# Router choices stored compactly and spread out by GpSimd in the expert stage, and router scores for two tiles at once

## What is computed

```python
logits = einsum('bgtd,des->bgtes', grouped, controller) + tie
perm = (logits == max(logits, axis=t))          # 1.0 or 0.0
dispatched = einsum('bgtd,bgtes->bgesd', grouped, perm)
inner = relu(einsum('bgesd,desf->bgesf', dispatched, f1) + bias)
intermediate = einsum('bgesf,esfd->bgesd', inner, f2)
out = einsum('bgesd,bgtes->bgtd', intermediate, perm)
x = layernorm(x + out)
```

## Time and profile before

| | us |
|---|---|
| median of 3 executions | 2290.38 |
| range of them | 2289.61 to 2296.89 |
| profiled execution, its own time | 2293.73 |
| its span, first to last instruction | 2291.9 |

### The profile page before, as it was taken

How to read it: one execution, slowest core, us unless ns; L and a number is a source line. 1 busy time by engine, 2 the same in 40 slices (tenths; PEclk the granted TensorE clock), 3 DMA queues, 4 the chain that set the end, 5 groups by cost and what they waited for, 6 DMA issues and landing times. The chain is left out here.

```text
span 2291.9 us, 35132 instructions
## 1 busy us (share of the span) xinstructions
PE 1934.8 (84%) x12598; PEld 1322.7 (58%) x12598; DVE 1405.0 (61%) x2695; ACT 940.8 (41%) x1751; POOL 443.1 (19%) x283
## 2 busy tenths in 40 slices
PE   7999999999999799999789999993767676576444
PEld 6777777777777343444378888883636362252000
DVE  5887778777877354555478889874434354354344
ACT  4444444444444344544345555552323232232222
POOL 1100100010000143554355554530000000000000
PEclk9999999999999899999989999995889887787555
DMA  5233333333422588887587777757798999989999
GB/s 169 74 122 118 113 109 132 112 111 111 138 102 93 171 221 231 222 222 221 158 259 245 239 243 222 238 169 258 248 389 290 390 348 407 404 305 408 375 392 345
DMA packets 306173, 522.66 MB, mean 228 GB/s; under 512 B 27119, under 2 KB 125583, under 8 KB 297682
## 3 DMA queue, kind: packets, MB, share of 16 engines
q1 hardware_dynamic: 296786, 503.63, 65.1%
q10 hardware_dynamic: 9216, 16.78, 1.9%
HBM read 314.50 MB, written 205.82 MB: 227 GB/s over the span
## 5 line engine op out<-in xcount | busy, mean ns | idle before, releaser
L89 PE MATMUL p_pu<-p_xT_high,p_win_high 128*128 128x512 f32 (+1 forms) x816 | 334.8, 410 | 13.5 <-DVE p_win_low L84 13.3
L91 PE MATMUL p_pu<-p_xT_low,p_win_high 128*128 128x512 f32 (+1 forms) x816 | 318.3, 390 | 0.0
L90 PE MATMUL p_pu<-p_xT_high,p_win_low 128*128 128x512 f32 (+1 forms) x816 | 318.3, 390 | 0.0
L422 ACT ACTIVATE p_t<-p_pu,p_tbias,p_taps 128x512 f32<-128x512 f32 x192 | 149.4, 778 | 383.4 <-PE p_pu L91 382.5
L536 DVE SCALAR_TENSOR_TENSOR p_t<-p_pu,p_taps,p_t 128x384 f32<-128x384 f32 (+1 forms) x384 | 210.3, 548 | 6.8
L808 POOL TENSOR_TENSOR q_y<-q_y 128x512 f32<-128x512 f32 x128 | 160.7, 1277 | 191.7 <-DVE q_y L829 191.7
L84 POOL TENSOR_TENSOR p_xT_low<-p_xT,p_xT_high 128x2048 fp32r<-128x2048 f32 (+1 forms) x17 | 75.8, 4458 | 616.7 <-ACT p_xT_high L79 616.7
L89 PEld LDWEIGHTS p_pu<-p_xT_high,p_win_high 128*128 128x128 f32 x816 | 155.0, 190 | 46.6 <-POOL p_xT_low L84 11.5
L91 PEld LDWEIGHTS p_pu<-p_xT_low,p_win_high 128*128 128x128 f32 x816 | 154.3, 189 | 34.3
L90 PEld LDWEIGHTS p_pu<-p_xT_high,p_win_low 128*128 128x128 f32 x816 | 155.1, 190 | 27.2
L1406 PE MATMUL e_pd<-e_taken,e_ff 128*32 128x128 f32 x2048 | 86.8, 324 | 96.7 <-DMA e_ff<-in_L_ffn_f 93.0
(11 more groups left out here) (123 smaller groups left out, 3754.1 us busy)
## 6 DMA issues: line engine op xcount, KB each, us to landing
s_I<-e_out SPq DMA_DIRECT2D x64, 1024.0 KB, 8.2
s_SV<-p_sout SPq DMA_DIRECT2D x128, 256.0 KB, 2.0
q_av<-s_SV SPq DMA_DIRECT2D x64, 512.0 KB, 4.3
s_Z<-q_z SPq DMA_DIRECT2D x128, 256.0 KB, 3.2
o_zin<-s_Z SPq DMA_DIRECT2D x64, 512.0 KB, 3.7
e_ff<-in_L_ffn_f SPq DMA_DIRECT2D x64, 512.0 KB, 9.0
e_inter<-s_I SPq DMA_DIRECT2D x32, 1024.0 KB, 12.8
e_taken<-s_I SPq DMA_DIRECT2D x32, 1024.0 KB, 11.7
```

The costliest lines, as they stand in the source:

```text
L89: pe.matmul(out, a[0], b[0], start=start, stop=False)
L90: pe.matmul(out, a[1], b[0], start=False, stop=False)
L91: return pe.matmul(out, a[0], b[1], start=False, stop=stop)
L422: nc.scalar.activation(t[r][m % 2][:], pu[(W + n) % 3][:], ACT.Identity, bias=tbias[:, w:w + 1], scale=taps[:, w, 2:3]).then_inc(t_ok, 1)
```

## The change

- `TOOK` is stored without the zeros, in an order in which one partition's values of four tiles lie together: shape (2, 128, 64, 64) instead of (8192, 2, 128), 4 MB. Each transposed block is copied once, unscaled: even v by ACT, odd v by DVE after the next unit's `choose`. A store is 256 KB in pieces of 1 KB.
- In the expert phase SP loads `picked`, the compact choices of four tiles (two pairs), 128 KB in pieces of 1 KB, into one of two buffers: the load for pairs j+3 and j+4 stands in SP's list at odd j, behind pair j+8. GpSimd makes the block-diagonal `pick` of each pair (NP = 3 buffers) by two multiplications with the columns of `side`, 128x128 each. PE waits for GpSimd (`pick_ok`) instead of the DMA.
- `side` is loaded in the expert phase instead of the frequency phase; DVE's and GpSimd's waits on `consts` are adjusted.
- `logits(q)` serves two tiles at once, four matmuls of 256 columns at every even n; `xT` and `pl` hold two tiles; `keep_logits` runs twice at even n.

```diff
@@ output_phase, sync
-                    for s in range(2):
-                        sp.wait_ge(took_ok[s], ONE + v + 1)
-                    sp.dma_start(td[v], took[v % NK][:].rearrange("p b h g e -> p b (h g e)")).then_inc(took_st[v % NK], 16)
+                    sp.wait_ge(took_ok[b], ONE + u + 1)
+                    sp.dma_start(S["TOOK"][:, :, 4 * v:4 * v + 4, :].rearrange("h p m e -> p h (m e)"),
+                                 took[v % NK][:].rearrange("p h m e -> p h (m e)")).then_inc(took_st[v % NK], 16)
@@ output_phase, tensor
-            def logits(n):
-                pe.wait_ge(xT_ok, ONE + n + 1)
-                pe.wait_ge(l_ok, ONE + n)
+            def logits(q):
+                pe.wait_ge(xT_ok, ONE + 2 * q + 2)
+                pe.wait_ge(l_ok, ONE + 2 * q)
                 for k in range(DT):
-                    m = pe.matmul(pl[:], ctrl[:, k, :], xT[n % 2][:, k, :], start=(k == 0), stop=(k == DT - 1))
+                    m = pe.matmul(pl[:].rearrange("p a t -> p (a t)"), ctrl[:, k, :],
+                                  xT[q % 2][:, k].rearrange("p a t -> p (a t)"), start=(k == 0), stop=(k == DT - 1))
                 m.then_inc(l_ps, 1)
-                if 0 <= n - 3 < TILES:
-                    logits(n - 3)
+                if 0 <= n - 3 < TILES and n % 2 == 0:
+                    logits((n - 3) // 2)
@@ output_phase, both copies
+        def keep_took(eng, copy, v):
+            eng.wait_ge(t_ps, ONE + v + 1)
+            if v >= NK:
+                eng.wait_ge(took_st[v % NK], ONE + v // NK * 16)
+            copy(took[v % NK][:].rearrange("p h b e -> p b h e"), pt[v % 2][:].rearrange("p b (h e) -> p b h e", h=2)
+                 ).then_inc(took_ok[v % 2], 1)
@@ experts_phase, sync
             def load_picks(w):
-                if w >= NP:
-                    sp.wait_ge(tile_ps, ONE + (w - NP + 1) * 2)
-                sp.dma_start(pick[w % NP][:], td[(c // 2) * PH + j, c % 2]).then_inc(pick_in[w % NP], 16)
+                c, q = w // NW, w % NW
+                if w >= 2:
+                    sp.wait_ge(pick_ok, ONE + (w - 1) * 2)
+                at = (c // 2) * TH + 4 * q
+                sp.dma_start(picked[w % 2][:], S["TOOK"][c % 2, :, at:at + 4, :]).then_inc(picked_in[w % 2], 16)
             for j in range(2):
+                load_picks(j)
                 load_pair(0, j)
-                load_picks(j)
...
-                    load_picks(c * PH + j + NP)
+                    if j % 2:
+                        load_picks(c * NW + j // 2 + 2)
@@ experts_phase, gpsimd
+            pool.wait_ge(consts, ONE + 32)
+            for n in range(STEPS * PH):
+                w = n // 2
+                pool.wait_ge(picked_in[w % 2], ONE + (w // 2 + 1) * 16)
+                if n >= NP:
+                    pool.wait_ge(tile_ps, ONE + (n - NP + 1) * 2)
+                for g in range(2):
+                    x = pool.tensor_scalar(pick[n % NP][:, :, g * EH:(g + 1) * EH], picked[w % 2][:, n % 2 * 2:n % 2 * 2 + 2, :],
+                                           side[:, g:g + 1], None, ALU.mult)
+                x.then_inc(pick_ok, 1)
@@ experts_phase, tensor
-                pe.wait_ge(pick_in[(c * PH + j) % NP], ONE + ((c * PH + j) // NP + 1) * 16)
+                pe.wait_ge(pick_ok, ONE + c * PH + j + 1)
```

More of the change, by code:

```diff
@@ L130, in output_tables @@
             "ident": sb("ident", [P, P]), "grow": sb("grow", [P, DT, P]), "grow_c": sb("grow_c", [P, DT, N2]),
-            "fbias": sb("fbias", [P, DT]), "bout": sb("bout", [P, D]), "side": sb("side", [P, 2]), "eps": sb("eps", [P, 1])}
+            "fbias": sb("fbias", [P, DT]), "bout": sb("bout", [P, D]), "eps": sb("eps", [P, 1])}
 def front_phase(nc, sem, A, S, F):
@@ L850, in ps @@
             return ctx.enter_context(nc.psum_tensor("o_" + name, shape, F32))
-        ctrl, ident, grow, grow_c, fbias, bout, eps, side, wout_s = (O[n] for n in (
-            "ctrl", "ident", "grow", "grow_c", "fbias", "bout", "eps", "side", "wout"))
+        ctrl, ident, grow, grow_c, fbias, bout, eps, wout_s = (O[n] for n in (
+            "ctrl", "ident", "grow", "grow_c", "fbias", "bout", "eps", "wout"))
         zin = [sb(f"zin{s}", [P, 2, D]) for s in range(NZ)]
@@ L865, in output_phase @@
         std = [sb(f"std{s}", [P, 1]) for s in range(2)]
-        xT = [sb(f"xT{s}", [P, DT, P]) for s in range(2)]
+        xT = [sb(f"xT{s}", [P, DT, 2, P]) for s in range(2)]
         logit = sb("logit", [P, N1, 2, GT])
         top = [sb(f"top{s}", [P, UG]) for s in range(2)]
-        took = [sb(f"took{s}", [P, 4, 2, 2, ES // 2]) for s in range(NK)]
+        took = [sb(f"took{s}", [P, 2, 4, ES // 2]) for s in range(NK)]
         pc = [ps(f"pc{s}", [P, DT, P]) for s in range(2)]
@@ L1011, in turn_take @@
                 if v >= 2:
-                    for s in range(2):
-                        pe.wait_ge(took_ok[s], ONE + v - 1)
+                    pe.wait_ge(took_ok[v % 2], ONE + v // 2)
                 for b in range(4):
@@ L1052, in keep_x @@
                 act.wait_ge(x_turned, ONE + n + 1)
[L1053 to L1062, removed]
+                if n >= 4:
+                    act.wait_ge(l_ps, ONE + n // 2 - 1)
+                nc.scalar.copy(xT[n // 2 % 2][:, :, n % 2, :], px[:]).then_inc(xT_ok, 1)
             def high_y(n):
@@ L1082, in _ @@
                     finish(n - 1)
-            for v in range(2 * UNITS):
-                keep_took(v)
+            for u in range(UNITS):
+                keep_took(act, nc.scalar.copy, 2 * u)
         @block.vector
@@ L1127, in keep_logits @@
             def keep_logits(n):
-                dve.wait_ge(l_ps, ONE + n + 1)
-                dve.tensor_scalar(logit[:, :, n // HALF, n % HALF], pl[:], float(tie[n % HALF]), None, ALU.add
+                dve.wait_ge(l_ps, ONE + n // 2 + 1)
+                dve.tensor_scalar(logit[:, :, n // HALF, n % HALF], pl[:, n % 2], float(tie[n % HALF]), None, ALU.add
                                   ).then_inc(l_ok, 1)
[L1132 to L1137, removed]
             def choose(u):
@@ L1157, in _ @@
                     moments(n)
-                if 0 <= n - 3 < TILES:
-                    keep_logits(n - 3)
+                if 0 <= n - 3 < TILES and n % 2 == 0:
+                    for a in range(2):
+                        keep_logits(n - 4 + a)
                 for u in chosen(n):
@@ L1162, in _ @@
                     if u > UNITS:
[L1163 to L1166, removed]
+                        keep_took(dve, dve.tensor_copy, 2 * (u - UNITS - 1) + 1)
+            keep_took(dve, dve.tensor_copy, 2 * UNITS - 1)
 def experts_phase(nc, sem, A, S):
@@ L1182, in experts_phase @@
     NX = 8
-    NP = 4
+    NP = 3
+    NW = TH // 4
     IN_DISPATCH = (3, 6, 9, 12, 15)
@@ L1198, in experts_phase @@
         pick = [sb(f"pick{s}", [P, 2, 2 * EH]) for s in range(NP)]
+        picked = [sb(f"picked{s}", [P, 4, EH]) for s in range(2)]
+        side = sb("side", [P, 2])
         ff = [sb(f"ff{s}", [P, 2, D]) for s in range(NF)]
@@ L1216, in experts_phase @@
         pair_in = [sem(f"e_pair_in{s}") for s in range(NX)]
-        pick_in = [sem(f"e_pick_in{s}") for s in range(NP)]
+        picked_in, pick_ok = [sem(f"e_picked_in{s}") for s in range(2)], sem("e_pick_ok")
         tile_ps, taken_ok = sem("e_tile_ps"), [sem(f"e_taken_ok{s}") for s in range(2)]
@@ L1266, in _ @@
         def _(sp):
+            sp.dma_start(side[:], A["side"]).then_inc(consts, 16)
             sp.dma_start(bias[:], A["ffn_bias"]).then_inc(consts, 16)
```

16 lines of the change are left out of this document (5 added, 11 removed).

## The result

| | before | after |
|---|---|---|
| median of 20 executions, us | 2288.99 | 2294.01 |
| lowest and highest | 2283.81, 2296.89 | 2286.30, 2298.71 |
| span of the profiled execution | 2291.9 | 2295.1 |

A forecast was written before the change was run, and what follows sets the result against it. PE was taken to bound the output tiles, DMA stores that stage's end, and late loads of choices the dispatches. Terms -11.5 - 1.6 + 4.4 + 4.0 + 2.0 = -2.7 gave 2287.5 us, range 2275 to 2301.

The forecast's parts named there:

- the sum of the dispatches: Expert stage: +4.4 us in c=0, +4.0 in c=1, about +1 each in c=2 and c=3.
- Scores for two tiles: Output stage tiles: eight records of 256 columns replace two times eight of 128, 32 times; -1.6 us, ends -4 and +3.
- eight of 256 take 1.72: Output stage tiles: at 0.84 ns a column the scores take 1.72 us instead of 1.76, gaining 0.04 to 0.05 a pair.
- Stores of the choices: End of the output stage: 16 stores halve, 4.19 MB less for full DMA engines; -11.5 us, ends -3.5 and -12.5.
- Rival C: End of the output stage: buffers wait for landed stores, so that part gains only 3.5 us; 2295.5 us, chance 0.08.
- the freed DMA time: Dispatches: lighter loads of choices free 5.6 us of DMA time per step c, worth time only where PE waits for the queue.
- The remark that at line rate the sum would be 1 us lower: Dispatches: if GpSimd ran its one-input multiplications near line rate, the forecast sum would be about 1 us lower.
- the 0.85: Dispatches: GpSimd's two multiplications at 0.35 us each plus semaphores, 0.85 us between landing and matmul.
- 1.86 us a pair: Dispatches: time a pair costs when nothing is late, from four pairs in 7.45 us.
- the forecast's 3.8 us at pair 8: Dispatch of c=0: the load of choices for pair 8 lands in 3.8 us in a drained queue; wait +1.5 us.
- Rival B: Dispatches: shorter lead, loads landing at 6.0 us at pairs 8 and 12, c=2 and 3 at +4 each; 2300 us, chance 0.23.
- Rival A: Dispatches: loads of choices land within 3.1 us, new waits vanish, c=2 and 3 gain 2 each; 2277 us, chance 0.24.

The follow-up runs named there:

- scores2: The kernel before with router scores for two tiles in one go and nothing else; 2280.2 us against 2291.5, ratio 0.9948.
- early: The kernel after with each load of choices issued as soon as its buffer is free, ahead of the pair; 2249.2 us, ratio 0.9809 to the kernel before.

## Why the prediction was wrong

It named the two sides of the change and where each would show, but its sum, -2.7, was a small difference of large terms, and most of the terms were too small. The step that turned the sign is the sum of the dispatches, +10.4 where +25.1 was measured. That the total still came within 7 us of the forecast is luck: the output stage was forecast some 10 us too small, the dispatches 15, and these errors partly cancel.

*Scores for two tiles: forecast -1.6, measured -11.* The step that failed is "eight of 256 take 1.72 ... gain 0.04 to 0.05 a pair". The eight records take 1.542 us where two times eight took 1.770, so the scores alone gain 0.23 a pair (these are medians over the steady tiles); the price of 0.84 ns a column, read from matmuls of 512 columns in another stage, didn't hold here. What stands next to the scores was left out. `conv` takes 1.706 us in the tile without scores and 1.787 in the other, where it took 1.812 before in both, which gives 0.13. The first record of `out` takes 0.42 behind the longer scores instead of 0.32, which costs 0.10. Together that is the 0.26 of the pair period. The last tile, with its wait for DVE, wasn't looked at, and gave 3 more. The lower end of the range for this term (-4) didn't reach it either.

*Stores of the choices: forecast -11.5, measured -13.5* (scores2 and after differ by that at the first matmul, 1590.0 and 1576.5). The mechanism was right: the stage lasts as long as its stores. Rival C is out, since landing fell with the queue and the DMA share stayed at 0.96.

*Dispatches: forecast +10.4, measured +25.1.* The places were right: pairs 4, 8 and 12 in c=0 and 1. The sizes were not.

| | forecast | measured | of it waits | of it slower matmuls |
|---|---|---|---|---|
| c=0 | +4.4 | +5.7 | +5.7 | +0.1 |
| c=1 | +4.0 | +10.5 | +7.1 | +3.4 |
| c=2 | +1 | +5.7 | +5.3 | +0.3 |
| c=3 | +1 | +3.2 | +2.5 | +0.7 |

Most of the miss, 10 of 15 us, is in the waits. The largest part of that is c=2 and 3, where the freed DMA time was to give most of the loss back. The prediction named one wait there, of 2.73 us; the kernel before has 7.5 us of them in c=2 and 7.6 in c=3. The largest of c=2, before pair 4, grew from 4.21 to 7.63; these are the rows before and after:

```profile
1847.42 2.93 PE L1394 MATMUL e_pd<-e_pick,e_out 64*128 64x128 f32 x24 [4.21 <-issue]
```

```profile
1840.81 8.54 PE L1398 MATMUL e_pd<-e_pick,e_out 64*128 64x128 f32 x96 [7.63 <-issue]
```

GpSimd is in these waits too: 0.35 us an operation was taken and 0.60 came, so the step behind a landing is 1.3 to 1.4 us and not 0.85, half a microsecond more at each wait. (The remark that at line rate the sum would be 1 us lower doesn't follow from the terms either: the 0.85 stands in eight of them. The trace has 0.60 for one input, and that decides.) One term was missing from the sum altogether, the clock. Behind the waits of 6 to 8 us in c=0 and 1 four pairs ran at a mean clock of 0.73 to 0.78 and took 9.3 to 9.9 us instead of 7.4, while the forecast had 1.86 us a pair throughout. The length of the wait alone does not decide it: four pairs behind the wait of 2.09 took 9.0 us, at 0.81. Slower matmuls made 4.5 of the 25 us, 3.4 of them in c=1; in c=0 the kernel before lost as much to them.

*Landing, the forecast's 3.8 us at pair 8:* 4.5 in c=0 and 3.9 in c=1. Rival B came out on the right side, and its +4 each for c=2 and 3 was near (+5.7, +3.2). Its mechanism for c=0 and 1, landing at 6.0 at pairs 8 and 12, did not happen at pair 8, nor at pair 12 of c=1 (4.8); the shorter lead was the cause, but by way of the reasons above. Rival A needed landing under 3.1. (The section of the Trainium skill that the prediction cites for the 2.3 us of this rival, DMA: Bandwidth & Descriptors, Anatomy of one DMA, is on DMAs that GpSimd issues, while SP issues these; with nothing ahead they landed in 2.1 us in both kernels.)

That the lead was the term to look at is shown, not argued: taking one pair of lead from the kernel before costs 24 us, giving it back to the kernel after wins 23. How the gain of early divides between more lead and the place ahead of the pair was not tried; in the kernel before the place alone was worth 10. The split of a dispatch's loss into waits and slower matmuls was read from single executions, and no run holds the clock still. The 3.1 us in the rest of the expert stage are spread over layers and last combines and stay unexplained.

## What to carry to other kernels

When a load is made to serve two uses, count how far ahead of its first use it can still be issued, and what stands in front of it in its queue: a lead of 3.7 us against landings of 4 to 10 cost more here than halving the bytes won. Put the small load that an engine will need next ahead of the big ones it will need later, and let it go as soon as its own buffer is free, not when the big load's is. And where a forecast is the difference of two large terms, their errors decide it; measure each by itself before trusting the sign.

## What the runs showed that was not expected

- Two multiplications on GpSimd with a per-partition factor took 602 ns each for 128 elements a partition. Its two-input additions in the kernel before, 1277 ns for 512 and 4458 for 2048 elements, lead by a straight line to 480 for 128. (The 4458 is the mean of a group with one smaller addition in it; the 16 of 2048 elements take 4590, which gives 450.)
- The first split (float32r) matmul record behind float32 ones takes longer: 0.32 us to the next record behind records of 128 columns, 0.42 behind those of 256, against 0.235 afterwards. Scores in half as many, twice as long, pieces were worth 0.26 us a pair of tiles in spite of it.
- Turning round two neighbouring DMA issues, 128 KB ahead of 512 KB, was worth 10 us of 2290 in the kernel before.
- The fastest kernel here keeps the whole change and alters only the order of SP's list: 2239.8 us, 2.1% below before, where the change as it was made is 0.2% above.
- Of the 25 us that the dispatches lost, 4.5 were slower matmuls. The kernel before had pairs at a lower clock behind its own waits as well, so a longer wait in the same place added no more of them in c=0.
